# Reordering the last two output tiles of a two-layer graph kernel, and storing one of them through GpSimd's queue

## The chip, the cores and the metric

The kernel runs on one core of a Trainium2 chip. A core has five engines that each work through their own list of instructions: TensorE (PE, matrix products), VectorE (DVE), ScalarE (ACT), GpSimd (POOL) and SyncE (SP, which here only issues transfers). They wait for each other through semaphores. Transfers between the on-chip memory and the chip's main memory are issued from the queues of SP, ACT or POOL and are carried by 16 DMA engines. The metric is the device time of one execution in microseconds (us); less is better.

## The reference, cut to what matters

```python
def _layernorm(x, axis=-1, eps=1e-05):
    m = jnp.mean(x, axis=axis, keepdims=True)
    v = jnp.var(x, axis=axis, keepdims=True)
    return (x - m) / jnp.sqrt(v + eps)

# x: (1354, 512), adj: (1354, 1354), 0/1 with the diagonal set
def _L0_gnn_ref(inst_feature, aggregator_matrix, rel_pair_index, Wq, bq, Wk, bk):
    ...                      # attention scores at 10000 listed pairs, masked by adj, softmax over rows
    return aggregator_factor @ inst_feature

def _L1_gnn_ref(x, adj, weight, bias):
    support = jnp.matmul(x, weight)
    output = jnp.matmul(adj, support)
    return output + bias

x = _layernorm(x + _L0_gnn_ref(x, adj, ...), axis=-1)
x = _layernorm(x + _L1_gnn_ref(x, adj, weight, bias), axis=-1)
```

Everything that this case is about lies in the last line: the sum with the residual `x`, and the normalisation of each row of 512 numbers.

## The kernel before, in words

The 1354 rows are cut into `T` = 11 tiles of `P` = 128 rows (the last has 74), each 512 wide (`H`). The first layer, the handling of the listed pairs and the product of the first layer's result with `adj` fill the first 127 us. Then the output loop starts. It goes over the tiles in the order `OUT_ORDER` = 0 to 4, 10, 5 to 9; in what follows a tile is called by its place in that order, so that "the last tile" is place 10 and "the last but one" is place 9.

For each tile, TensorE makes 12 products with the weights and one that corrects and adds the bias (`weigh`, L1462, and `correct`, L1483). The last tile is cut into columns 0 to 319 and 320 to 511 (`LAST_PARTS`), so that VectorE can start on the first part while TensorE makes the second.

VectorE then does for each tile (L1256 to L1262): the sum with the residual (SCALAR_TENSOR_TENSOR), the statistics (BATCH_NORM_STATS2), and their mean and variance (BATCH_NORM_AGGREGATE). ScalarE takes the root of the variance plus eps (L713). VectorE takes the reciprocal of the root (L905) and multiplies it with minus the mean (L906): these two are `finish_stats`, which gives the scale and the shift. ScalarE normalises the tile in place as scale times value plus shift (L812), and SP issues the store of the tile (L607). ScalarE thus alternates: root of tile t, normalisation of tile t. VectorE calls `finish_stats(t - 1)` after the statistics of tile t.

At the end this differs. For the last tile VectorE makes the sum and the statistics of its first part, then `finish_stats` of the last but one tile (L1276), then the sum and statistics of the second part, the mean and variance (L1279), and `finish_stats` of the last tile (L1280). The last tile is normalised by two engines at once: columns 0 to 255 by ScalarE (L812), columns 256 to 511 by VectorE (L1283). It is stored in two halves of 64 rows, one issued by SP (L610), one by ScalarE (L816). SP at last waits for all stores to land.

GpSimd takes no part in the output loop. Its last work is the scatter of 64 corrected rows (L690), at 121 us; all its transfers before are indirect gathers and scatters (rows chosen by an index).

The buffers of the output tiles are four (`y4`: two halves of `y`, two of `xd`), the statistics sit in `st`, which has two places, taken in turn.

Of the kernel before, what the change touches and what calls it, by code (L numbers as in the profile page):

```python
# [39 lines left out]
BACK_BEFORE = {0: 0, 2: 1, 5: 2, 6: 3}  # L40
SPANS = [(0, 512), (512, 1024), (1024, N)]
UNITS = KF * len(SPANS)
HALF = H // 2
LAST_PARTS = ((0, 320), (320, H))
OUTS = 6
EARLY = 2
# [14 lines left out]
def resnorm_graph(nc, x, adj, pairs, pairs_left, b_qk, w1, b1, adj_t, adj_cols, wq_t, wk_t, adj_diag, out):  # L61
# [5 lines left out]
    with ExitStack() as ctx:  # L67
# [3 lines left out]
        def sem(name):  # L71
            return ctx.enter_context(nc.semaphore(name))
# [180 lines left out]
        qk_read, change_ready, change_T, dT_hi, dT_lo = map(sem, ("qk_read", "change_ready", "change_T", "dT_hi", "dT_lo"))  # L253
        dS_done, right_hi, right_lo = map(sem, ("dS_done", "right_hi", "right_lo"))
        bias_row_loaded, bias_split, biased, ones_laid, out_done, z_ready, z_moments, z_root = map(sem, ("bias_row_loaded", "bias_split", "biased", "ones_laid", "out_done", "z_ready", "z_moments", "z_root"))
        z_stats, z_normed, z_half_normed = map(sem, ("z_stats", "z_normed", "z_half_normed"))

        map_clear, map_idx_ready, map_zeroed, map_marked = map(sem, ("map_clear", "map_idx_ready", "map_zeroed", "map_marked"))
        general_in, rows_in, general_step, early_read = map(sem, ("general_in", "rows_in", "general_step", "early_read"))

        turn = sem("turn")
        out_stored = [sem(f"out_stored{i}") for i in range(4)]
        last_stored = [sem(f"last_stored{i}") for i in range(2)]

        block = ctx.enter_context(nc.Block())

# [21 lines left out]
        def unless_few(eng, name, count, ahead, general):  # L288

            eng.br_lt(count, CAP + 1, on_true=name + "_few", on_false=name + "_many").branch_hint(ahead)  # L290
            with nc.body(name + "_many", valid_engines=[eng.engine]):
                general(eng)
                eng.br(name + "_few")
            nc.switch_bb(name + "_few")
# [235 lines left out]
        def y4(t):  # L530

            return (y if t % 4 < 2 else xd)[:, t % 2, :]
# [9 lines left out]
        @block.sync  # L542
        def _(sp):
            sp.dma_start(ed_i[:], pairs.rearrange("(p c) two -> p c two", p=EP)).then_inc(edges_loaded, 16)
            for g, (a, b) in enumerate(FIRST_PARTS):
                sp.dma_start(stage[:, 0:2, a * P:b * P],  # L546
                             adj_t[0:2].rearrange("t p c -> p t c")[:, :, a * P:b * P]).then_inc(first_loaded[g], 16)
                if g < 3:
                    sp.dma_start(x_sb[:, a:b, :], x[a * P:b * P, :].rearrange("(t p) h -> p t h", p=P)).then_inc(x_loaded[g], 16)
            sp.dma_start(x_sb[:, T - 2, :], rows(x, T - 2)).then_inc(x_loaded[3], 16)  # L550
            sp.dma_start(x_sb[0:64, T - 1, :], x[(T - 1) * P:(T - 1) * P + 64, :]).then_inc(x_loaded[3], 16)
            sp.wait_ge(pad_zeroed, 1)
            sp.dma_start(x_sb[64:LAST, T - 1, :], x[(T - 1) * P + 64:N, :]).then_inc(x_loaded[3], 16)

            def load_adj(t):
                if t >= RING + 2:
                    sp.wait_ge(adj_cast, t - RING - 1)
                elif t >= RING:
                    sp.wait_ge(first_cast, len(FIRST_PARTS))
                sp.dma_start(stage[:, t % RING, :], adj_t[t]).then_inc(adj_loaded[t % RING], 16)  # L560

            load_adj(2)
            sp.wait_ge(edges_split, 2)
            sp.dma_start(row_dram.rearrange("(c p) -> c p", c=LEFT), row16[:]).then_inc(row_stored, 16)
            sp.dma_start(col_dram.rearrange("(c p) -> c p", c=LEFT), col8[:]).then_inc(col_stored, 16)
            load_adj(3)
            load_adj(4)
            load_adj(5)
            load_adj(6)
            sp.wait_ge(row_stored, 16)  # L570
            sp.dma_start(hot[:, :], row_dram.partition_broadcast(P)).then_inc(row_spread, 16)
            load_adj(7)
            sp.wait_ge(col_stored, 16)
            sp.dma_start(cols[:, :], col_dram.partition_broadcast(P)).then_inc(col_spread, 16)
            for t in range(8, T):
                load_adj(t)
            sp.dma_start(bias_row[:, :], b1.rearrange("(o h) -> o h", o=1)).then_inc(bias_row_loaded, 16)
            sp.dma_start(bias_col[:, :, :], b_qk).then_inc(bias_loaded, 16)
            sp.wait_ge(adj_cast, T - 2)
            sp.dma_start(w1_raw, w1.rearrange("(k p) o -> p k o", p=P)).then_inc(w1_loaded, 16)  # L580
            sp.dma_start(wT[:, 0], wq_t.rearrange("(k p) o -> p k o", p=P)).then_inc(wq_loaded, 16)
            sp.dma_start(wT[:, 1], wk_t.rearrange("(k p) o -> p k o", p=P)).then_inc(wk_loaded, 16)
            ahead = sp.mark_branch_hint_location()
            for half in range(2):
                sp.dma_start(adj_tail[EVEN * half:EVEN * half + EVEN, 0:N], adjT[0:EVEN, T - 1, 0:N]).then_inc(tail_laid, 16)
            for t in range(T):
                sp.wait_ge(x1_ready, t + 1)
                sp.dma_start(rows(x1_dram, t), x_sb[0:width[t], t, :]).then_inc(x1_stored, 16)
            sp.wait_ge(odd_zeroed, 1)
            sp.dma_start(x1_odd[CAP:BIAS_ROW, :], x_sb[EVEN:LAST, T - 1, :]).then_inc(odd_in, 16)  # L590
            sp.wait_ge(ones_laid, 1)
            for half in range(2):
                sp.dma_start(stackL[SLOTS * half + CAP:SLOTS * half + BIAS_ROW, 0:N], adjT[EVEN:LAST, T - 1, 0:N]).then_inc(odd_laid, 16)
            sp.wait_ge(bias_split, 2)
            for half in range(2):
                at = SLOTS * half + BIAS_ROW
                sp.dma_start(stackR[at:at + 1, :], bias_hl[:, half, :]).then_inc(biased, 16)
            sp.wait_ge(x1_scattered, 16)
            for n, (a, b) in enumerate(BACK_PARTS):
                if b < T:  # L600
                    sp.dma_start(x_sb[:, a:b, :], x1_dram[a * P:b * P, :].rearrange("(t p) h -> p t h", p=P)).then_inc(x1_back[n], 16)
                else:
                    sp.dma_start(x_sb[0:LAST, a, :], rows(x1_dram, a)).then_inc(x1_back[n], 16)
            unless_few(sp, "sp", slots_wanted(sp), ahead, general_sp)
            for n, t in enumerate(OUT_ORDER[:-1]):
                sp.wait_ge(z_normed, n + 1)
                sp.dma_start(rows(out, t), y4(n)[0:width[t]]).then_inc(out_stored[n % 4], 16)  # L607
            sp.wait_ge(z_normed, T)
            sp.wait_ge(z_half_normed, 1)
            sp.dma_start(rows(out, OUT_ORDER[-1])[0:64, :], y4(T - 1)[0:64, :]).then_inc(last_stored[0], 16)  # L610
            for b in range(4):
                sp.wait_ge(out_stored[b], 16 * len(range(b, T - 1, 4)))
            for half in range(2):
                sp.wait_ge(last_stored[half], 16)


        @block.gpsimd
        def _(pool):
# [73 lines left out]
                in_=q[0:SLOTS, :], in_offset=None, bounds_check=N - 1, oob_is_err=False).then_inc(x1_scattered, 16)  # L692
            pool.wait_ge(x1_scattered, 16)
            unless_few(pool, "pool", slots_wanted(pool), ahead, general_pool)


        @block.scalar
        def _(act):
# [105 lines left out]
            mix_high(11)  # L804
            unless_few(act, "act", slots_wanted(act), ahead, general_act)

            for t in range(T):
                act.wait_ge(z_moments, t + 1)
                root(st[:, t % 2], eps[:]).then_inc(z_root, 1)
                act.wait_ge(z_stats, t + 1)  # L810
                part = y4(t) if t < T - 1 else y4(t)[:, 0:HALF]
                nc.scalar.activation(part, part, ACT.Identity, bias=st[:, t % 2, 9:10],  # L812
                                     scale=st[:, t % 2, 8:9]).then_inc(z_normed, 1)
            act.wait_ge(z_normed, T)
            act.wait_ge(z_half_normed, 1)
            act.dma_start(rows(out, OUT_ORDER[-1])[64:P, :], y4(T - 1)[64:P, :]).then_inc(last_stored[1], 16)  # L816


# [1 line left out]
        def _(dve):  # L820
# [445 lines left out]
            for n, (a, b) in enumerate(LAST_PARTS):  # L1266
                part = y4(t)[:, a:b]
                dve.wait_ge(out_done, T + n)
                V.scalar_tensor_tensor(part, last_bank(n)[:, 0:b - a], 1.0 / WS, x_sb[:, OUT_ORDER[t], a:b],
                                       ALU.mult, ALU.add).then_inc(z_ready, 1)  # L1270
                dve.wait_ge(z_ready, T + n)
                ins = V.bn_stats(last_st[:, 6 * n:6 * n + 6], part)
                if n == 0:
                    ins.then_inc(dve_step, 1)
                    steps += 1
                    finish_stats(T - 2)  # L1276
            step(ins)
            dve.wait_ge(z_normed, t - 1)
            V.bn_aggr(st[:, t % 2, 6:8], last_st[:, 0:12]).then_inc(z_moments, 1)  # L1279
            finish_stats(t)  # L1280
            dve.wait_ge(z_stats, T)
            part = y4(t)[:, HALF:H]
            V.tensor_scalar(part, part, st[:, t % 2, 8:9], st[:, t % 2, 9:10], ALU.mult, ALU.add).then_inc(z_half_normed, 1)  # L1283


        @block.tensor
# [261 lines left out]
```

## Time and profile before

| | us |
|---|---|
| median of 3 runs | 166.4 |
| the 3 runs | 166.4, 167.87, 165.41 |
| the profiled execution's own time | 166.01 |
| its span, from the first to the last instruction | 164.3 |
| granted TensorE clock, mean over the span | 0.991 of full speed |
| busy: TensorE, VectorE, ScalarE, GpSimd | 154.7, 124.5, 74.9, 68.6 |

A line of the timeline reads: start, duration, engine, line of the program, operation, output and input by name, shape, how many; in brackets how long the engine was idle before it and who released it. "SPq" and "ACTq" are issues of transfers on a queue; their duration is that of the issue, not of the transfer. A line of the list of transfers ends with the KB of one and the time from its issue to its landing. A line of the table by stretch gives the stretch, its length, the busy time of PE, PE's weight load, DVE, ACT and POOL with the number of instructions, the granted TensorE clock, the busy share of the DMA engines and the GB/s that they moved. The names `y` and `xd` are output tiles, `st` and `last_st` are statistics, `acc` and `tr` are banks in which TensorE leaves its sums.

### The profile page before, as it was taken

Reading aid. Unit: us, or ns where it says so; the run is one execution under the profiler, and the core shown is the slowest. Engines: PE = TensorE matmul, PEld = TensorE weight load, DVE = VectorE, ACT = ScalarE, POOL = GpSimd, SP = SyncE. Lnnn points to the kernel's source line nnn. Section 1 sums busy time; section 2 is a strip of 40 time slices with the busy share of each in tenths; the row PEclk is TensorE's granted clock in tenths of the full one; section 3 lists DMA queues with packets and bytes.
Section 4 is the critical chain, followed back from the end, with each engine's and each line's share of the span. In section 5 each row is a group of like instructions: output and inputs, shape, how many; then the busy total and the mean of one; then the engine's idle time right before and its main releaser. Section 6 shows DMA issues by size and latency. Waiting matters only on the chain.

```text
span 164.3 us, 2912 instructions
## 1 busy us (share of the span) xinstructions
PE 154.7 (94%) x1029; PEld 81.5 (50%) x1029; DVE 124.5 (76%) x391; ACT 74.9 (46%) x126; POOL 68.6 (42%) x83
## 2 busy tenths in 40 slices
PE   3999999999999999999999999999999999999940
PEld 3964444555454445444454485445764444444530
DVE  2876689997799999999678786898981368666681
ACT  5586639855874312864291253061211204333451
POOL 7787777777777777777306233000030000000000
PEclk9999999999999999999999999999999999999996
DMA  5999979999249999651003720000002972311234
GB/s 126 369 385 335 322 241 363 392 411 339 79 119 345 353 339 394 207 131 42 0 0 94 193 92 6 0 0 0 0 14 51 364 253 86 132 75 66 88 128 128
DMA packets 16232, 28.99 MB, mean 176 GB/s; under 512 B 4769, under 2 KB 5953, under 8 KB 16086
## 3 DMA queue, kind: packets, MB, share of 16 engines
q1 hardware_dynamic: 10742, 24.14, 41.7%
q10 hardware_dynamic: 3280, 3.07, 5.7%
q0 software_dynamic: 2192, 1.57, 4.1%
q8 instruction: 9, 0.15, 0.4%
q14 instruction: 9, 0.07, 0.1%
HBM read 19.83 MB, written 8.58 MB: 173 GB/s over the span
## 4 chain that ended last, share of the span: by engine, by line
PE 61%; DMA 12%; DVE 12%; ACT 6%; SPq 4%; issue 2%; ACTq 0%; DVEq 0%
PE acc L1379 23%; PE acc L1467 13%; PE acc L1311 9%; DMA stage<-in_adj_T 6%; DMA x_sb<-in_x 6%; ACT adjT L702 3%; PE tr L1467 3%; PE tr L1311 3%; DVE st L900 2%; PE tr L1421 2%; PE tr L1457 2%; SPq L546 1%; PE acc L1383 1%; PE acc L1492 1%; PE tr L1325 1%
## 5 line engine op out<-in xcount | busy, mean ns | idle before, releaser
L651 POOL DMA_INDIRECT ed_adj<-in_adj,ed_idx x47 | 47.0, 1001 | 14.5 <-issue 14.0
L1379 PE MATMUL acc<-adjT,x1s 128*128 128x512 f16 (+1 forms) x240 | 49.2, 354 | 0.0
L1311 PE MATMUL acc<-xs,adjT 128*128 128x512 f16 (+1 forms) x176 | 40.2, 379 | 0.0
L1379 PEld LDWEIGHTS acc<-adjT,x1s 128*128 128x128 f16 x240 | 22.7, 98 | 21.1 <-issue 0.2
L1311 PEld LDWEIGHTS acc<-xs,adjT 128*128 128x128 f16 (+1 forms) x176 | 16.5, 98 | 18.9 <-ACT xs L718 0.4
L1467 PE MATMUL acc<-whl,xs 128*128 128x512 f16 (+1 forms) x108 | 23.8, 370 | 0.0
L1467 PEld LDWEIGHTS acc<-whl,xs 128*128 128x128 f16 x108 | 10.6, 98 | 11.8
L1311 PE MATMUL tr<-xs,adjT 128*128 128x512 f16 (+1 forms) x66 | 15.2, 379 | 0.0
L702 ACT CAST adjT<-stage 128x1408 f16<-128x1408 f32 x9 | 12.3, 1361 | 4.0 <-DMA stage<-in_adj_T 3.6
L755 ACT ACTIVATE xs<-acc 128x512 f16<-128x512 f32 (+1 forms) x12 | 6.2, 538 | 9.6 <-PE acc L1383 9.6
L690 POOL DMA_INDIRECT x_dram<-wraw,back_i x1 | 1.3, 1337 | 21.3 <-DVE wraw L1229 21.3
L1311 PEld LDWEIGHTS tr<-xs,adjT 128*128 128x128 f16 (+1 forms) x66 | 6.3, 98 | 7.3
L659 POOL DMA_INDIRECT found<-in_adj,top_i x8 | 8.6, 1070 | 3.0 <-issue 2.1
L873 DVE SCALAR_TENSOR_TENSOR xs<-x_sb,xs 128x512 f16<-128x512 f32 x11 | 7.0, 684 | 3.6 <-ACT xs L718 3.6
L713 ACT ACTIVATE st<-st,co 128x1 f32<-128x1 f32 x11 | 3.2, 292 | 14.0 <-DVE st L901 14.0
L713 ACT ACTIVATE st<-st,eps 128x1 f32<-128x1 f32 x13 | 3.7, 284 | 12.9 <-DVE st L901 12.8
L1292 PE MATMUL tr<-ones 128*128 128x128 f16 x72 | 6.4, 277 | 2.8 <-POOL row_no L632 2.8
L1256 DVE SCALAR_TENSOR_TENSOR y<-acc,x_sb 128x512 f32<-128x512 f32 x5 | 3.5, 692 | 7.1 <-PE acc L1492 7.1
L812 ACT ACTIVATE y<-y,st 128x512 f32<-128x512 f32 x6 | 4.9, 813 | 8.6 <-DVE st L906 8.6
L900 DVE BATCH_NORM_STATS2 st<-y 128x6 f32<-128x512 f32 x12 | 8.3, 695 | 0.4
L718 ACT ACTIVATE xs<-x_sb 128x512 f16<-128x512 f32 x11 | 6.2, 619 | 4.3 <-DMA x_sb<-in_x 4.3
L925 DVE SCALAR_TENSOR_TENSOR xs<-acc,xs 128x512 f16<-128x512 f32 (+1 forms) x12 | 7.2, 619 | 0.9 <-ACT xs L755 0.7
(279 smaller groups left out, 230.7 us busy)
## 6 DMA issues: line engine op xcount, KB each, us to landing
stage<-in_adj_T SPq DMA_DIRECT2D x9, 704.0 KB, 6.5
x_dram<-x_sb SPq DMA_DIRECT2D x10, 256.0 KB
x_sb<-in_x SPq DMA_DIRECT2D x3, 768.0 KB, 7.7
sums_dram<-y ACTq DMA_DIRECT2D x6, 256.0 KB
sums_dram<-xd ACTq DMA_DIRECT2D x5, 256.0 KB, 7.1
x_sb<-x_dram SPq DMA_DIRECT2D x1, 1280.0 KB, 11.8
out<-y SPq DMA_DIRECT2D x5, 256.0 KB, 2.0
stage<-in_adj_T SPq DMA_DIRECT2D x3, 384.0 KB, 5.9
```

Source lines behind the costliest of these rows:

```text
L651: nc.gpsimd.indirect_dma_start(out=ed_adj[0:EP, c:c + 1], out_offset=None, in_=adj_flat, in_offset=bass.IndirectOffsetOnAxis(ap=ed_idx[0:E ...
L659: nc.gpsimd.indirect_dma_start(out=found[0:EP, c:c + 1], out_offset=None, in_=adj_flat, in_offset=bass.IndirectOffsetOnAxis(ap=top_i[0:EP, ...
L702: nc.scalar.copy(adjT[:, :, t * P:(t + 1) * P], stage[:, t % RING, :].rearrange("p (k i) -> p k i", k=T)).then_inc(adj_cast, 1)
L713: return nc.scalar.activation(s[:, 10:11], s[:, 7:8], ACT.Sqrt, bias=floor)
L718: nc.scalar.mul(xs[:, 0, t, :], x_sb[:, t, :], XS).then_inc(x_hi, 1)
L873: V.scalar_tensor_tensor(xs[:, 1, t, :], x_sb[:, t, :], XS, xs[:, 0, t, :], ALU.mult, ALU.subtract).then_inc(x_lo, 1)
L900: step(V.bn_stats(s[:, 0:6], v))
L925: V.scalar_tensor_tensor(mix[:, 1, u % KF, i:j], mix_bank(u)[:, 0:j - i], 1.0 / XS, mix[:, 0, u % KF, i:j], ALU.mult, ALU.subtract).then_i ...
L1292: mm(tr[2][:, 0:P], ones16[:], ones16[:], start=True, stop=True)
L1311: last = mm(sum_bank(i)[:, :], adjT[0:width[k], k, i * P:(i + 1) * P], xs[0:width[k], half, k, :], start=(k == 0 and half == 0), stop=(k = ...
L1379: mm(mix_bank(u)[:, 0:j - i], x1s[:, half, k, f * P:(f + 1) * P], adjT[:, k, i:j], start=(k == 0 and half == 0), stop=False)
L1467: last = mm(bank, mix[:, a, k, t * P:(t + 1) * P], whl[:, b, k, columns], start=(k == 0 and m == 0), stop=False)
```

## The change

Five things change, all in the output loop's end.

VectorE makes the last tile's second sum directly after the first part's statistics; `finish_stats` of the last but one tile goes behind the last tile's mean and variance. The last tile gets no shift any more: VectorE waits for its root, takes the reciprocal and normalises all 512 columns by itself as (value minus mean) times reciprocal. ScalarE takes both last roots first and then normalises the last but one tile, and leaves the last tile alone. The store of the last but one tile goes from SP's queue to GpSimd's. SP and ScalarE still store half of the last tile's rows each.

```diff
@@ SP
-            for n, t in enumerate(OUT_ORDER[:-1]):
+            for n, t in enumerate(OUT_ORDER[:-2]):
                 sp.wait_ge(z_normed, n + 1)
                 sp.dma_start(rows(out, t), y4(n)[0:width[t]]).then_inc(out_stored[n % 4], 16)
-            sp.wait_ge(z_normed, T)
-            sp.wait_ge(z_half_normed, 1)
+            sp.wait_ge(z_last_normed, 1)
             sp.dma_start(rows(out, OUT_ORDER[-1])[0:64, :], y4(T - 1)[0:64, :]).then_inc(last_stored[0], 16)
             for b in range(4):
-                sp.wait_ge(out_stored[b], 16 * len(range(b, T - 1, 4)))
-            for half in range(2):
-                sp.wait_ge(last_stored[half], 16)
+                sp.wait_ge(out_stored[b], 16 * len(range(b, T - 2, 4)))
+            for n in range(3):
+                sp.wait_ge(last_stored[n], 16)
@@ GpSimd
             unless_few(pool, "pool", slots_wanted(pool), ahead, general_pool)
+            n, t = T - 2, OUT_ORDER[T - 2]
+            pool.wait_ge(z_normed, n + 1)
+            nc.gpsimd.dma_start(rows(out, t), y4(n)[0:width[t]]).then_inc(last_stored[2], 16)
@@ ScalarE
-            for t in range(T):
+            def z_root_of(t):
                 act.wait_ge(z_moments, t + 1)
                 root(st[:, t % 2], eps[:]).then_inc(z_root, 1)
+
+            def z_norm_of(t):
                 act.wait_ge(z_stats, t + 1)
-                part = y4(t) if t < T - 1 else y4(t)[:, 0:HALF]
-                nc.scalar.activation(part, part, ACT.Identity, bias=st[:, t % 2, 9:10],
+                nc.scalar.activation(y4(t), y4(t), ACT.Identity, bias=st[:, t % 2, 9:10],
                                      scale=st[:, t % 2, 8:9]).then_inc(z_normed, 1)
-            act.wait_ge(z_normed, T)
-            act.wait_ge(z_half_normed, 1)
+
+            for t in range(T - 2):
+                z_root_of(t)
+                z_norm_of(t)
+            z_root_of(T - 2)
+            z_root_of(T - 1)
+            z_norm_of(T - 2)
+            act.wait_ge(z_last_normed, 1)
             act.dma_start(rows(out, OUT_ORDER[-1])[64:P, :], y4(T - 1)[64:P, :]).then_inc(last_stored[1], 16)
@@ VectorE
                 if n == 0:
                     ins.then_inc(dve_step, 1)
                     steps += 1
-                    finish_stats(T - 2)
             step(ins)
             dve.wait_ge(z_normed, t - 1)
             V.bn_aggr(st[:, t % 2, 6:8], last_st[:, 0:12]).then_inc(z_moments, 1)
-            finish_stats(t)
-            dve.wait_ge(z_stats, T)
-            part = y4(t)[:, HALF:H]
-            V.tensor_scalar(part, part, st[:, t % 2, 8:9], st[:, t % 2, 9:10], ALU.mult, ALU.add).then_inc(z_half_normed, 1)
+            finish_stats(T - 2)
+            dve.wait_ge(z_root, T)
+            step(V.reciprocal(st[:, t % 2, 8:9], st[:, t % 2, 10:11]))
+            V.tensor_scalar(y4(t), y4(t), st[:, t % 2, 6:7], st[:, t % 2, 8:9], ALU.subtract, ALU.mult).then_inc(z_last_normed, 1)
```

VectorE, from the last tile's first sum to the end of its list. `xd` is the last tile, `last_st` its statistics, `acc` and `tr` the banks of its two parts. Before:

```order
L1269 SCALAR_TENSOR_TENSOR xd<-acc,x_sb 128x320 [waits out_done,out_stored2]
L1272 BN_STATS last_st<-xd 128x6 [waits z_ready]
L905 RECIPROCAL st<-st 128x1 [waits z_root]
L906 TENSOR_SCALAR st<-st 128x1 [waits dve_step]
L1269 SCALAR_TENSOR_TENSOR xd<-tr,x_sb 128x192 [waits out_done]
L1272 BN_STATS last_st<-xd 128x6 [waits z_ready]
L1279 BN_AGGR st<-last_st 128x2 [waits z_normed,dve_step]
L905 RECIPROCAL st<-st 128x1 [waits z_root]
L906 TENSOR_SCALAR st<-st 128x1 [waits dve_step]
L1283 TENSOR_SCALAR xd<-xd,st 128x256 [waits z_stats]
```

After, in the changed program's own line numbers:

```order
L1277 SCALAR_TENSOR_TENSOR xd<-acc,x_sb 128x320 [waits out_done,out_stored2]
L1280 BN_STATS last_st<-xd 128x6 [waits z_ready]
L1277 SCALAR_TENSOR_TENSOR xd<-tr,x_sb 128x192 [waits out_done]
L1280 BN_STATS last_st<-xd 128x6 [waits z_ready]
L1286 BN_AGGR st<-last_st 128x2 [waits z_normed,dve_step]
L913 RECIPROCAL st<-st 128x1 [waits z_root]
L914 TENSOR_SCALAR st<-st 128x1 [waits dve_step]
L1289 RECIPROCAL st<-st 128x1 [waits z_root]
L1290 TENSOR_SCALAR xd<-xd,st 128x512 [waits dve_step]
```

The last but one tile's reciprocal and shift moved from before the second sum to behind the last tile's mean and variance; the last tile's own shift is gone, and its normalisation covers 512 columns.

ScalarE, from the last but one tile's root to the end. Before:

```order
L713 ACTIVATE st<-st,eps 128x1 [waits z_moments]
L812 ACTIVATE y<-y,st 128x512 [waits z_stats]
L713 ACTIVATE st<-st,eps 128x1 [waits z_moments]
L812 ACTIVATE xd<-xd,st 128x256 [waits z_stats]
L816 DMA out<-xd 64x512 [waits z_half_normed,z_normed]
```

After:

```order
L714 ACTIVATE st<-st,eps 128x1 [waits z_moments] x2
L814 ACTIVATE y<-y,st 128x512 [waits z_stats]
L824 DMA out<-xd 64x512 [waits z_last_normed]
```

Both roots now stand ahead of the last but one tile's normalisation (`y`), and the normalisation of the last tile (`xd`) left this engine.

## Rows read from the trace of the kernel before

**Rows 1.** The page: busy time, share and instructions of each engine.

```profile
PE 154.7 (94%) x1029; PEld 81.5 (50%) x1029; DVE 124.5 (76%) x391; ACT 74.9 (46%) x126; POOL 68.6 (42%) x83
```

**Rows 2.** The page: the chain that ended last, by engine.

```profile
PE 61%; DMA 12%; DVE 12%; ACT 6%; SPq 4%; issue 2%; ACTq 0%; DVEq 0%
```

**Rows 3.** Timeline from 157.2 us: the last two tiles.

```profile
157.27 0.81 ACT L812 ACTIVATE y<-y,st 128x512 f32<-128x512 f32 x1 [1.81 <-DVE st L906]
157.66 0.49 DVE L1272 BATCH_NORM_STATS2 last_st<-xd 128x6 f32<-128x320 f32 x1
...
157.85 0.25 PE L1492 MATMUL tr<-stackR,stackL 128*128 128x192 f16 x1
157.99 0.28 ACT L713 ACTIVATE st<-st,eps 128x1 f32<-128x1 f32 x1
...
158.30 0.17 DVE L905 RECIPROCAL st<-st 128x1 f32<-128x1 f32 x1
158.50 0.21 DVE L906 TENSOR_SCALAR st<-st 128x1 f32<-128x1 f32 x1
158.63 0.35 DVE L1269 SCALAR_TENSOR_TENSOR xd<-tr,x_sb 128x192 f32<-128x192 f32 x1
158.75 0.81 ACT L812 ACTIVATE y<-y,st 128x512 f32<-128x512 f32 x1 [0.48 <-DVE st L906]
159.01 0.36 DVE L1272 BATCH_NORM_STATS2 last_st<-xd 128x6 f32<-128x192 f32 x1
159.41 0.21 DVE L1279 BATCH_NORM_AGGREGATE st<-last_st 128x2 f32<-128x12 f32 x1
159.65 0.29 ACT L713 ACTIVATE st<-st,eps 128x1 f32<-128x1 f32 x1
159.98 0.17 DVE L905 RECIPROCAL st<-st 128x1 f32<-128x1 f32 x1 [0.36 <-ACT st L713]
160.18 0.21 DVE L906 TENSOR_SCALAR st<-st 128x1 f32<-128x1 f32 x1
160.43 0.60 ACT L812 ACTIVATE xd<-xd,st 128x256 f32<-128x256 f32 x1 [0.48 <-DVE st L906]
160.43 0.41 DVE L1283 TENSOR_SCALAR xd<-xd,st 128x256 f32<-128x256 f32 x1
161.05 0.56 SPq L610 DMA_DIRECT2D out<-xd  x1
161.06 0.56 ACTq L816 DMA_DIRECT2D out<-xd  x1
```

**Rows 4.** Timeline of SP's queue from 159.3 us: the last but one store.

```profile
159.59 0.33 SPq L607 DMA_DIRECT2D out<-y  x1
```

**Rows 5.** Transfers: direction, queue, kind, count, KB of one, us to landing.

```profile
out<-y SPq DMA_DIRECT2D x5, 256.0 KB, 2.0
...
out<-xd SPq DMA_DIRECT2D x1, 128.0 KB, 2.4
out<-xd ACTq DMA_DIRECT2D x1, 128.0 KB, 2.7
...
wraw<-sums_dram,slot_i POOLq DMA_INDIRECT x1, 3.9
```

**Rows 6.** By stretch: the last but one store's data on the DMA engines.

```profile
160.80:161.10 0.30, 0.00 (x0) 0.00 (x0) 0.04 (x1) 0.23 (x1) 0.00 (x0) 1.00 0.95 375
```

**Rows 7.** Timeline, 86 to 88 us: GpSimd's first gather of rows.

```profile
86.67 0.17 DVE L1085 CAST slot_i<-slot 128x2 int32<-128x2 f32 x1
87.11 0.94 POOL L664 DMA_INDIRECT wraw<-in_x,slot_i  x1 [7.83 <-DVE slot_i L1085]
```

**Rows 8.** That gather's line (128 rows of 2 KB): time from issue to landing.

```profile
DMA to landing us min/median/max: 3.3/3.3/3.3
```

**Rows 9.** Timeline, 119 to 122 us: GpSimd's scatter and its releaser.

```profile
119.66 0.55 DVE L1229 TENSOR_SCALAR wraw<-wraw,st 128x512 f32<-128x512 f32 x1
...
121.19 1.34 POOL L690 DMA_INDIRECT x_dram<-wraw,back_i  x1 [21.27 <-DVE wraw L1229]
```

More of the change, by code:

```diff
@@ L42 @@
 UNITS = KF * len(SPANS)
-HALF = H // 2
 LAST_PARTS = ((0, 320), (320, H))
@@ L255, in resnorm_graph @@
         bias_row_loaded, bias_split, biased, ones_laid, out_done, z_ready, z_moments, z_root = map(sem, ("bias_row_loaded", "bias_split", "biased", "ones_laid", "out_done", "z_ready", "z_moments", "z_root"))
-        z_stats, z_normed, z_half_normed = map(sem, ("z_stats", "z_normed", "z_half_normed"))
+        z_stats, z_normed, z_last_normed = map(sem, ("z_stats", "z_normed", "z_last_normed"))
         map_clear, map_idx_ready, map_zeroed, map_marked = map(sem, ("map_clear", "map_idx_ready", "map_zeroed", "map_marked"))
@@ L262, in resnorm_graph @@
         out_stored = [sem(f"out_stored{i}") for i in range(4)]
-        last_stored = [sem(f"last_stored{i}") for i in range(2)]
+        last_stored = [sem(f"last_stored{i}") for i in range(3)]
         block = ctx.enter_context(nc.Block())
```

## The prediction

> **What bounds the kernel now.** I read the busy shares first: TensorE is busy for 154.7 of 164.3 us, 94% [rows 1], so for most of the span nothing but TensorE counts, and the change doesn't touch it. The chain of waits says the same with one addition: TensorE has 61% of it, VectorE 12% and ScalarE 6% [rows 2]. So VectorE and ScalarE count only where TensorE has nothing left to do. The timeline shows that place. TensorE's last product ends at 157.85 + 0.25 = 158.10 us [rows 3], and the span ends at 164.3 us. The last 6.2 us are a tail without TensorE, and the whole change lies in it. Whatever it does is worth a part of 6.2 us in 166, that is at most 3.7%, and nothing that any row suggests comes near that.
>
> The tail has two pieces. The first is a chain of small instructions on VectorE and ScalarE, up to 161.05 us, where SP and ScalarE issue the two halves of the last tile's store [rows 3]. The second is the store itself: ScalarE's half takes longer, 2.7 us to landing [rows 5], so it lands at 161.06 + 2.7 = 163.76 us. From there to the end of the span are 0.54 us, in which SP's last wait falls and the program ends; I keep these 0.54 us behind whichever store lands last. The reader should see one more thing in the rows: the last but one tile is normalised at 158.75 + 0.81 = 159.56 us and its store goes out at 159.59 us [rows 3, 4]. With 2.0 us to landing [rows 5] it is down at 161.59 us, over 2 us before the end. This tile has slack before, and the change spends it.
>
> **The second sum moves ahead.** Before, it starts at 158.63 us, behind a reciprocal that had to wait for ScalarE's root (157.99 + 0.28 = 158.27) and a shift. Without these two it can start when the first part's statistics end, 157.66 + 0.49 = 158.15, and when TensorE's last product is there, 158.10 [rows 3]. With the 0.02 us that the rows show between dependent instructions I take 158.17: 0.46 us earlier. TensorE stands right behind this: were VectorE earlier still, nothing would be gained.
>
> The rest of the chain keeps the distances of rows 3. Statistics 0.38 us behind the sum: 158.55. Mean and variance 0.40 behind that: 158.95. The root 0.24 behind: 159.19. ScalarE is free by then, since its last root ended at 158.27 and no normalisation stands between any more. The mean and variance also wait for the normalisation that ends at 157.27 + 0.81 = 158.08; it has long ended. The reciprocal comes 0.33 behind the root, at 159.52.
>
> **The last tile's shift goes, VectorE normalises alone.** Before, from reciprocal to shift 0.20 us, from shift to normalisation 0.25 us, and ScalarE's half took 0.60 us, VectorE's 0.41 us, so ScalarE's set the end [rows 3]. Now the normalisation follows the reciprocal by the 0.20 us that a step on VectorE takes: 159.72. It has 512 columns. A row of the same operation, shape and two scalars from memory took 0.55 us [rows 9]; that is no guess between bounds, though it would be 0.82 us if twice the 256 columns took twice the time. So it ends at 160.27, and the stores go out 0.02 later at 160.29 us, against 161.05: 0.76 us earlier, of which 0.46 came from the sum, 0.25 from the shift, and 0.05 from 0.55 against 0.60 us. ScalarE's issue has to go behind its normalisation of the other tile, below, and so at 160.34 us at the worst; I leave this 0.05 us in the rounding. With 2.7 us to landing the last tile is down at 162.99 us.
>
> **The last but one tile.** Its reciprocal and shift go behind the last tile's mean and variance. An independent instruction follows at 0.13 us (the sum behind the shift, 158.50 to 158.63), so the reciprocal is at 159.08, the shift 0.20 later at 159.28, and it ends at 159.49, just before 159.52, where the last tile's reciprocal wants VectorE. It is hidden under ScalarE's root; if that cover is missed by the 0.03 us that is left, it costs as much. ScalarE's normalisation starts 0.25 behind the shift, at 159.53 (its second root ends at 159.48), and ends at 160.34 us, 0.78 us later than before.
>
> **Its store through GpSimd.** This is the term that no row shows: GpSimd has issued only indirect transfers. Two durations are needed. From the release to the start of the issue: 0.27 us at the first gather (86.67 + 0.17 to 87.11 [rows 7]), 0.98 us at the scatter (119.66 + 0.55 to 121.19 [rows 9]); at best nothing. From the start to landing: a gather of the same 256 KB in rows of 2 KB took 3.3 us [rows 8], another 3.9 us, and a store of 256 KB from SP's queue 2.0 us [rows 5]. A gain below 2.0 us is excluded, since the bytes are the same and go the same way. I take the nearest rows, both from the one gather that found GpSimd idle, as this store will: 0.27 + 3.3 = 3.57 us. The bounds are 2.0 and 0.98 + 3.9 = 4.88 us. The store lands at 160.34 + 3.57 = 163.91 us.
>
> The three stores share the DMA engines. These moved 375 GB/s while the last but one store's data passed before [rows 6], which makes 0.70 us for 256 KB. The last tile's data would be delayed by that at most, to 163.69 us, still ahead of GpSimd's store; and I expect no overlap, for GpSimd's data should come later.
>
> **The sum.** The later landing is 163.91 us; with 0.54 us the span is 164.45 us, 0.15 us more than before. The 0.76 us won on the last tile are spent by the last but one, whose landing takes over the end. Against the profiled execution's own 166.01 us this gives **166.2 us**. That execution is 0.4 us below the median of the three runs, 166.4 us, and the three spread over 2.5 us (165.41 to 167.87), more than the whole effect. About 2%, 3.3 us, is what a measurement of this kernel can tell from no change.
>
> **Rival 1: GpSimd's store is quick and the last tile sets the end.** A plain store needs no index for each row, and the writing of descriptors, 0.94 us of the gather [rows 7], may shrink. For this to decide, release to landing must stay under 162.99 - 160.34 = 2.65 us. The span is then 162.99 + 0.54 = 163.53 us, the time 165.2 us. For it speaks that SP's plain store needs 2.0 us; against it, that every transfer of this queue with a landing shown took at least 3.3 us. The Trainium skill, page "DMA: Bandwidth & Descriptors", section "Latency and other measured facts", puts the first byte of a transfer of GpSimd's queue only some 0.4 us behind one of the other queues, and the section "Anatomy of one DMA — SWDGE (gpsimd) path" fits about 2.0 us plus the bytes at 436 GB/s: an estimate from that page is 2.6 us for these 256 KB, which would just fall under this rival. No row of this trace shows a plain store on that queue, and the gathers of rows 5 and 8 lie above it.
>
> **Rival 2: slower, because GpSimd wakes late and writes its descriptors late.** The place is the same store; the price is the other end of the bounds, 4.88 us, and it decides from 163.76 - 160.34 = 3.42 us on, where its landing passes that of before. Span 160.34 + 4.88 + 0.54 = 165.76 us, time 167.5 us, 0.9% slower. For it: the last transfer that GpSimd issued had this long start. Against: that row has an extra index bound to load ahead, and a scatter's descriptors took 1.34 us against 0.94 for a gather. My own forecast is the mild end of this mechanism, with 0.15 us past the threshold.
>
> **Rival 3: the move doesn't happen as drawn.** If TensorE's last product is seen by VectorE later than 158.10 (its ends are modelled), the second sum starts late by that; at 158.63, as before, the 0.46 us are gone. Then the last tile lands at 163.45, the last but one at 164.37, and the time is 166.6 us. The idle gaps after other tiles speak against it.
>
> **Chances.** The forecast (GpSimd's store sets the end, release to landing 3 to 4 us) has 0.45: nearest rows. Rival 1 has 0.27, rival 2 0.18, rival 3 0.06, and 0.04 is left for what I don't see, 0.02 beyond 2% on either side. Low end: rival 1's 165.2 less a little for the runs' spread, 165.1. High end: the forecast plus the spread of the runs above the profiled one, and the half of rival 2 up to 0.6% slower, 167.1. Faster by over 2% has 0.02, slower by over 2% 0.02 (it would take 164.3 + 3.3 - 0.54 - 160.34 = 6.7 us from release to landing), within 2% 0.96.
>
> **What the changed profile would show.** The second sum 0.02 us behind the first part's statistics, and no earlier than TensorE's last product. Reciprocal, shift, reciprocal on VectorE between the mean and variance and the root's return, without a gap that is longer than the 0.57 us of before. A normalisation of 512 columns of about 0.55 us, the stores of the last tile about 0.76 us earlier against TensorE's end, that is 2.2 us behind it. The last but one tile's normalisation ending within 0.1 us of the last one's. A GpSimd issue 0.3 us behind it, of about 0.9 us, and its landing as the last one. The prediction is wrong if SP's last wait ends on the last tile's halves (rival 1), if a GpSimd issue starts later than 0.5 us after its release or lands over 4 us behind (rival 2), or if ScalarE's store is held up behind its normalisation by more than 0.1 us.

## The result, and the profile after

| | before | after |
|---|---|---|
| median of 6 runs, us | 166.09 (165.41 to 168.22) | 169.24 (168.43 to 169.96) |
| ratio after to before | | 1.019, 95% interval 1.015 to 1.023 |
| span of the profiled execution, us | 164.3 | 167.3 |
| end of TensorE's last product, us | 158.10 | 158.26 |
| **tail**: from there to the end of the span, us | 6.2 | 9.04 |

The change makes the kernel slower by 1.9%, about 3.2 us. The forecast was 166.2 us with 165.1 to 167.1 as its range; the time lies outside. Of the 3.0 us by which the two spans differ, 0.16 us stand ahead of TensorE's end and 2.84 us in the tail. I use the tail for everything below, since what lies ahead of it moves from one execution to the next: the kernel before and e2_pool_only (below) run the same instructions up to there, and TensorE's last product ends at 158.10 us in one trace and at 160.14 us in the other. Each tail is read from one profiled execution; what repeats between kernels, as the 2.16 or 2.17 us to the last tile's stores, repeats within 0.01 us.

The timeline of the changed kernel's last two tiles answers to [rows 3]. Its columns are those of before; line numbers are those of the changed program.

```profile
157.82 0.49 DVE L1280 BATCH_NORM_STATS2 last_st<-xd 128x6 f32<-128x320 f32 x1
...
158.01 0.25 PE L1499 MATMUL tr<-stackR,stackL 128*128 128x192 f16 x1
...
158.29 0.36 DVE L1277 SCALAR_TENSOR_TENSOR xd<-tr,x_sb 128x192 f32<-128x192 f32 x1
158.69 0.36 DVE L1280 BATCH_NORM_STATS2 last_st<-xd 128x6 f32<-128x192 f32 x1
159.08 0.21 DVE L1286 BATCH_NORM_AGGREGATE st<-last_st 128x2 f32<-128x12 f32 x1
159.21 0.11 DVE L913 RECIPROCAL st<-st 128x1 f32<-128x1 f32 x1
159.32 0.29 ACT L714 ACTIVATE st<-st,eps 128x1 f32<-128x1 f32 x1 [0.90 <-DVE st L1286]
159.35 0.21 DVE L914 TENSOR_SCALAR st<-st 128x1 f32<-128x1 f32 x1
159.60 0.81 ACT L814 ACTIVATE y<-y,st 128x512 f32<-128x512 f32 x1
159.65 0.16 DVE L1289 RECIPROCAL st<-st 128x1 f32<-128x1 f32 x1
159.85 0.55 DVE L1290 TENSOR_SCALAR xd<-xd,st 128x512 f32<-128x512 f32 x1
160.42 0.56 SPq L608 DMA_DIRECT2D out<-xd  x1
160.43 0.57 ACTq L824 DMA_DIRECT2D out<-xd  x1
160.71 0.61 POOL L695 DMA_DIRECT2D out<-y  x1 [38.01 <-ACT y L814]
```

Up to the issues this is what was forecast: the last tile's stores go out 160.42 - 158.26 = 2.16 us behind TensorE's end, where before it was 161.05 - 158.10 = 2.95 us. So 0.79 us were won; the forecast had 0.76. What comes behind the issues ate them and more. First the landings, in the list of transfers of the changed kernel (it answers to [rows 5]; the last number is us from issue to landing):

```profile
out<-y POOLq DMA_DIRECT2D x1, 256.0 KB, 3.8
...
out<-xd SPq DMA_DIRECT2D x1, 128.0 KB, 2.7
out<-xd ACTq DMA_DIRECT2D x1, 128.0 KB, 4.2
```

GpSimd's store lands at 160.71 + 3.8 = 164.51 us, 6.25 us into the tail; the forecast had 5.81. ScalarE's half of the last tile, 2.7 us before, now needs 4.2 us: it lands at 164.63, the last of all. And from there to the end of the span are not 0.54 us but 2.7. The waits of SP's queue show that SP is done and waits for another engine at the program's end (engine and line that waited, what for, total us, times, longest):

```profile
SPq L612 <- DMA out<-xd: 3.6, 2, 2.2
SPq L66 <- PEq L66: 2.3, 1, 2.3
```

In the kernel before, the second of these waits was 0.2 us long. The row names TensorE's queue (PEq), but TensorE had long been done. Which engine it is, the line of the program's closing block tells. Its rows give the queue, the instruction, its length in ns (least, median, most), and when it starts. Before, L67:

```profile
L67 POOLq EVENT_SEMAPHORE  x2: 17/17/17, 164.1 to 164.2; - x2
L67 POOLq DRAIN  x1: 5042/5042/5042, 126.2 to 126.2; - x1
...
L67 ACTq DRAIN  x1: 646/646/646, 161.7 to 161.7; - x1
...
L67 SPq DRAIN  x1: 7/7/7, 164.0 to 164.0; - x1
```

After, L66:

```profile
L66 POOLq EVENT_SEMAPHORE  x2: 17/17/17, 167.1 to 167.2; - x2
...
L66 POOLq DRAIN  x1: 6372/6372/6372, 160.7 to 160.7; - x1
L66 ACTq DRAIN  x1: 645/645/645, 161.0 to 161.0; - x1
...
L66 SPq DRAIN  x1: 7/7/7, 165.0 to 165.0; - x1
```

Every engine closes its list with a DRAIN, and the closing EVENT_SEMAPHOREs of all come when the last DRAIN is through. GpSimd's takes 5.04 us. Before, GpSimd came to it at 126.2 us, and nobody noticed. After, GpSimd comes to it only with its store, at 160.7 us; it is through at 160.7 + 6.37 = 167.07, and the span ends at 167.3. SP's own drain began at 165.0. No row of the profile's page names a DRAIN; it shows only when the closing block's line is asked for.

### The profile page after: what moved, and what is told of

It reads as the page before. It is cut to its first block, busy times and chain, and to the rows that moved or that the text cites. A ratio compares the mean times of both kernels' runs of the same rounds, so it can differ in the third digit from the quotient of the medians.

```text
span 167.3 us, 2907 instructions
## 1 busy us (share of the span) xinstructions
PE 155.1 (93%) x1028; PEld 82.1 (49%) x1029; DVE 124.8 (75%) x390; ACT 74.3 (44%) x125; POOL 69.5 (42%) x84
## 4 chain that ended last, share of the span: by engine, by line
PE 46%; issue 25%; DVE 14%; POOL 5%; DMA 5%; POOLq 1%; DVEq 0%
PE acc L1318 17%; PE acc L1386 9%; PE tr L1318 9%; POOL found L657 4%; PE tr L1299 4%; DMA found<-in_adj,top_i 3%; PE tr L1304 2%; DMA x_dram<-wraw,back_i 2%; DVE st L908 2%; PE tr L1428 2%; DVE xs L933 1%; DVE y L957 1%; DVE hot L927 1%; PE tr L1332 1%; PE tr L1441 0%
## 5 line engine op out<-in xcount | busy, mean ns | idle before, releaser
L695 POOL DMA_DIRECT2D out<-y x1 | 0.6, 612 | 38.0 <-ACT y L814 38.0
L1299 PE MATMUL tr<-ones 128*128 128x128 f16 x72 | 7.1, 293 | 2.8 <-POOL row_no L630 2.8
L1299 PEld LDWEIGHTS tr<-ones 128*128 128x128 f16 x72 | 6.9, 140 | 2.8 <-POOL row_no L630 2.8
```

Source lines behind the costliest of these rows:

```text
L1299: mm(tr[2][:, 0:P], ones16[:], ones16[:], start=True, stop=True)
```

## The experiments

Theories at the start: **A**, GpSimd's closing drain costs about 5 us whenever it starts; **B**, it lasts until some 2.6 us behind the landing of GpSimd's store; **C**, the three stores get in each other's way, and the drain is only a shadow. All tails are read like that of the table above (start of TensorE's last product, plus its length, to the end of the span); "last tile issued" is the later of its issues, "landing" the latest one of all, issue plus time to landing; "drain ends" is GpSimd's closing one. All four are in us behind TensorE's end. Each ratio is to runs of the kernel before taken together with it.

| kernel | last tile issued | landing | drain ends | tail | ratio to before, 95% interval |
|---|---|---|---|---|---|
| before | 2.95 | 5.66 | long before | 6.2 | |
| after | 2.16 | 6.37 | 8.8 | 9.04 | 1.019 (1.015 to 1.023) |
| e1_sp_store | 2.55 | 5.35 | long before | 6.0 | 0.999 (0.995 to 1.002) |
| e2_pool_only | 2.95 | 5.65 | 7.5 | 7.66 | 1.008 (1.004 to 1.012) |
| e3_late_memset | 2.55 | 5.35 | 7.3 | 7.56 | 1.005 (1.001 to 1.009) |
| e4_wait_landing | 2.16 | 6.36 | 11.5 | 11.74 | one run |
| e5_early_drain | 2.17 | 6.27 | 6.2 | 6.83 | 1.004 (1.001 to 1.007) |
| e6_early_drain_memset | 2.56 | 5.36 | 2.4 | 5.99 | one run |
| e8_whole_stores | 2.17 | 4.88 | long before | 5.31 | 0.995 (0.992 to 0.998) |
| e9_pool_earlier | 2.16 | 4.88 | 3.2 | 5.39 | 0.995 (0.992 to 0.999) |
| e10_drain_count | 2.17 | 4.89 | long before | 5.34 | one run |
| e11_two_stores_drain | 2.16 | 5.05 | 5.2 | 5.61 | 0.998 (0.995 to 1.002) |
| e12_pool_only_drain | 2.95 | 5.65 | 4.3 | 6.24 | 0.999 (0.995 to 1.002) |
| e13_halves_one_queue | 2.77 | 6.47 | 6.4 | 7.01 | one run |

Runs of one kernel scatter by 1.3 to 2.5 us. The ratios part e2 from e1, but e3 from neither of them; the intervals agree with the tails (1.46 us more tail in e2 are 0.9%), and the tails carry the verdicts. All the experiments differ from the kernel before by less than 1%; where there is one run only, its time says nothing and its tail alone is used.

**e1_sp_store**, against the changed kernel:

```diff
 # SP
+            sp.wait_ge(z_normed, T - 1)
+            sp.dma_start(rows(out, OUT_ORDER[T - 2]), y4(T - 2)[0:width[OUT_ORDER[T - 2]]]).then_inc(last_stored[2], 16)
             sp.wait_ge(z_last_normed, 1)
 # GpSimd
-            pool.wait_ge(z_normed, n + 1)
-            nc.gpsimd.dma_start(rows(out, t), y4(n)[0:width[t]]).then_inc(last_stored[2], 16)
```

> The changed kernel with the last but one tile's store back on SP's queue, ahead of SP's half of the last tile; GpSimd does nothing in the output loop. The measure is the tail, from the end of TensorE's last product to the end of the span: 6.2 us before, 9.0 us with the change. Theory A (the closing drain on GpSimd's list holds the end, 6.4 us behind its store) and theory B (that drain ends some 2.6 us behind the landing of GpSimd's store) both expect a tail of about 5.6 us: GpSimd's drain is over long before, SP issues at 2.2 and 2.5 us, lands 2.4 to 2.7 us later, 0.5 us of ending. About 0.6 us faster than before. Theory C (the three stores are in each other's way, and ScalarE's half lands 4.2 us behind its issue because of it) expects 4.2 us to landing here too and a tail of 6.9 us.

Measured: tail 6.0 us. The loss is gone with GpSimd's store, so the new order on VectorE and ScalarE is not its cause. Only 0.2 us of the expected 0.6 are left as a gain: SP's half of the last tile is issued behind the other store at 2.55 us and takes 2.8 us to land. ScalarE's half lands in 2.8 us, not 4.2, although three stores cross here as well:

```profile
out<-xd ACTq DMA_DIRECT2D x1, 128.0 KB, 2.8
out<-xd SPq DMA_DIRECT2D x1, 128.0 KB, 2.8
```

Three stores on the queues of SP and ScalarE don't explain the 4.2, so C in its simple form is wrong.

**e2_pool_only**, the kernel before with one edit, the last but one tile's store on GpSimd's queue.

> The kernel before with one edit: the last but one tile's store goes from SP's queue to GpSimd's; VectorE and ScalarE as before. The tile is ready at 1.5 us of the tail, GpSimd issues at 1.8. Theories A and B: the drain ends 6.4 us behind that, a tail of 8.3 us, about 2.1 us slower than before, although this store lands (3.8 us behind its issue, at 5.6) no later than the last tile's. Theory C: the stores don't meet as closely, tail 6.2 to 6.7 us.

Measured: tail 7.66 us, 1.46 us more than before. ScalarE's half lands when it did, in 2.7 us, and GpSimd's store ahead of it:

```profile
out<-y POOLq DMA_DIRECT2D x1, 256.0 KB, 2.4
```

The drain ends 7.5 us into the tail. Here the drain is the whole loss. I had expected 8.3, as the drain took 6.37 us with the change; it takes 5.70 us here:

```profile
L67 POOLq DRAIN  x1: 5701/5701/5701, 161.9 to 161.9; - x1
```

Its row starts with the store's own issue, which takes GpSimd 0.61 us, so 5.09 us are left for the drain alone, against 5.76 with the change.

**e3_late_memset**, e1_sp_store with late work on GpSimd that is no transfer:

```diff
 # GpSimd, at its end
+            pool.wait_ge(z_normed, T - 1)
+            nc.gpsimd.memset(probe[:], 0.0)
```

> As e1_sp_store, but GpSimd waits for the last but one tile's normalisation and then sets 128 numbers of a scratch tile to zero: late work on GpSimd, no transfer. Theory A (the drain costs about 5 us whenever it starts, as in the trace of before where nothing was in flight): it starts at 2.2 us of the tail and ends at 7.3, tail 7.5 us, 1.9 us longer than e1_sp_store. Theory B (the drain waits for transfers): nothing is in flight, tail as e1_sp_store, 5.6 us.

```profile
163.75 0.10 POOL L697 MEMSET probe<- 128x1 f32 x1 [37.80 <-ACT y L816]
```

```profile
L66 POOLq DRAIN  x1: 5103/5103/5103, 163.7 to 163.7; - x1
```

Measured: tail 7.56 us against 7.5 (A) and 5.6 (B). The first row is of the timeline, the second of the closing block. One memset of 0.10 us costs 1.56 us at the end, with no transfer of GpSimd in flight for 38 us. B is wrong. (This profiled execution took 170.83 us against a median of 167.32; TensorE ended late in it, and only distances in its tail are used. The medians of e3 and e1, 167.32 and 166.15 us, differ the same way, by 1.2 us.)

**e4_wait_landing**, the changed kernel with `pool.wait_ge(last_stored[2], 16)` behind GpSimd's store.

> The changed kernel, with GpSimd waiting for its own store to land before it comes to the end of its list. The store lands at 6.3 us of the tail. Theory A: a drain of 5.0 us starts only then, tail 11.5 us, 2.5 us longer than with the change. Theory B: the drain has nothing left to wait for but the same 2.6 us behind the landing, tail 9.0 us as with the change; or, if that rest is not part of waiting, 7 us.

```profile
L66 POOLq DRAIN  x1: 5057/5057/5057, 165.8 to 165.8; - x1
```

Measured: tail 11.74 us. The store has landed when the drain starts, and the drain takes its 5.06 us all the same. A holds where nothing is in flight: the drain's start sets the end.

**e5_early_drain** and **e6_early_drain_memset** ask what these 5 us are paid for: for having issued transfers at all (A1), or for those issued since the last drain (A2). Both add one line behind GpSimd's scatter at 126 us, the first to the changed kernel, the second to e3_late_memset:

```diff
             unless_few(pool, "pool", slots_wanted(pool), ahead, general_pool)
+            nc.gpsimd.drain()
```

> The changed kernel with an extra drain on GpSimd at 126 us, right after its last gather and scatter work, where nothing waits for it. Theory A1 (a drain costs 5 us once GpSimd has issued any transfer in the program): the closing drain stays at about 5.7 us behind the store's descriptors, tail 9.0 us as with the change. Theory A2 (a drain pays for the transfers issued since the last drain; before, 60 of them): the closing drain has one store to pay for, so little more than its landing: tail about 7 us, 2 us less than with the change.

> e3_late_memset with the same extra drain at 126 us. Between the two drains GpSimd issues no transfer at all. A1: the closing drain takes 5.0 to 5.1 us again, tail 7.7 us. A2: it takes 0.2 us, like the one at the program's start (0.18 us), tail 5.9 us.

The closing block of e5_early_drain, then its extra drain (L693); under it the two of e6_early_drain_memset:

```profile
L66 POOLq DRAIN  x1: 3781/3781/3781, 160.5 to 160.5; - x1
...
L693 POOLq DRAIN  x1: 5047/5047/5047, 126.8 to 126.8; - x1
```

```profile
L66 POOLq DRAIN  x1: 173/173/173, 159.7 to 159.7; - x1
...
L696 POOLq DRAIN  x1: 5041/5041/5041, 125.4 to 125.4; - x1
```

A2 holds. In e6 the early drain takes the 5.04 us, and the closing one 0.17 us. In e5 the closing one has one store behind it and is through at 160.5 + 3.78 = 164.3 us, as that store lands (160.53 + 3.7 = 164.23). It is so in e11, e12 and e13 too, where the closing drain ends 0.1 us behind that landing. The tail falls from 9.04 to 6.83 us. One hidden instruction takes back 2.2 of the 2.84 us.

**e10_drain_count** has the extra drain between GpSimd's 55 lookups and its last 5 transfers; the rest is e8_whole_stores, below.

> e8_whole_stores with a drain on GpSimd behind the 47 and 8 lookups and ahead of its 5 last transfers (two gathers of rows, the gather of sums, the gather of columns, the scatter). Theory D1 (the cost goes with the number of transfers since the last drain): this drain takes some 4.6 us, plus what the last lookup still needs to land, and the closing one 0.17 + 5 x 0.08 = 0.6 us. D2 (any transfer since the last drain costs the whole 5 us): both take about 5.0 us. D3 (the cost is that of the gathers with long rows or of the scatter, not of the lookups): the first is short, the closing one near 5 us. The tail is that of e8_whole_stores, 5.3 us, in all three.

```profile
L66 POOLq DRAIN  x1: 529/529/529, 128.2 to 128.2; - x1
...
L661 POOLq DRAIN  x1: 16451/16451/16451, 69.4 to 69.4; - x1
```

D1: with 5 transfers since the last drain the closing one takes 0.53 us (expected 0.6), with 60 it takes 5.04, with none 0.17. That is (5.04 - 0.53) / 55 = 0.08 us for each transfer and (0.53 - 0.17) / 5 = 0.07, though the 5 move far longer rows than the 55; so it isn't the bytes. Each lookup addresses 128 rows and the last 5 transfers 64 or 128, so that a price for each transfer and a price for each row can't be told apart here. The first drain's row starts with the queue of lookups and can't be read for its price.

**e12_pool_only_drain**, e2_pool_only with the early drain.

> e2_pool_only with the extra drain at 126 us. The store of the last but one tile is issued by GpSimd at 1.8 us of the tail and lands at 4.2, the last tile's at 5.6 as in the kernel before. Theory A2 (a drain pays for the transfers since the last one, and waits for its own to land): the closing drain ends at the landing, 4.2, nothing is behind it, and the tail is 6.2 us as before: the 1.5 us that e2_pool_only lost are all the drain's.

Measured: tail 6.24 us against 6.2 expected. With the drain paid for early, moving the store to GpSimd costs nothing here, where 1.2 us lie between its issue and those of the halves, and GpSimd's store lands in 2.4 us.

**e8_whole_stores** goes after the landing, and for a better kernel. Against the changed one, GpSimd stores nothing, and:

```diff
 # SP
-            sp.dma_start(rows(out, OUT_ORDER[-1])[0:64, :], y4(T - 1)[0:64, :]).then_inc(last_stored[0], 16)
+            sp.dma_start(rows(out, OUT_ORDER[-1]), y4(T - 1)[0:P, :]).then_inc(last_stored[0], 16)
 # ScalarE
-            act.wait_ge(z_last_normed, 1)
-            act.dma_start(rows(out, OUT_ORDER[-1])[64:P, :], y4(T - 1)[64:P, :]).then_inc(last_stored[1], 16)
+            act.wait_ge(z_normed, T - 1)
+            act.dma_start(rows(out, OUT_ORDER[T - 2]), y4(T - 2)[0:width[OUT_ORDER[T - 2]]]).then_inc(last_stored[1], 16)
```

> The changed kernel with both last stores on the hardware queues, each whole: SP stores the last tile, ScalarE the last but one; GpSimd stores nothing. Issues at 2.2 us of the tail on both. If only GpSimd's drain and its store's crossing with the others cost time, the landing is some 2.9 us later (512 KB at 340 to 375 GB/s are 1.4 to 1.5 us) and the tail is 5.6 us, 0.6 us less than before and 3.4 less than with the change. If the three-store crossing of e1_sp_store is about bytes and not queues, the tail is 6.0 us as there.

Measured: tail 5.31 us (5.6 expected), 0.9 us less than before, ratio 0.995 with an interval clear of 1, by median 165.64 against 166.30 us. It has the shortest tail of this study; e9_pool_earlier, below, is as fast by its runs. The new order on VectorE and ScalarE is worth its gain once both stores are whole and on the queues of SP and ScalarE. Against e1_sp_store, which has the same order, the latest landing is 0.47 us earlier (4.88 against 5.35), of which 0.38 is the last issue: no store stands behind another. The issue rows tell part of it: a store of 128 rows takes SP 0.33 us to issue, one of 64 rows 0.56 (with the change, above). And whole tiles move faster. By stretch of 0.4 us (the last three numbers: TensorE's clock, busy share of the DMA engines, GB/s), the changed kernel:

```profile
161.46:161.86 0.40, 0.00 (x0) 0.00 (x0) 0.00 (x0) 0.00 (x0) 0.00 (x0) 1.00 0.61 138
161.86:162.26 0.40, 0.00 (x0) 0.00 (x0) 0.00 (x0) 0.00 (x0) 0.00 (x0) 1.00 1.04 154
162.26:162.66 0.40, 0.00 (x0) 0.00 (x0) 0.00 (x0) 0.00 (x0) 0.00 (x0) 0.75 0.76 215
162.66:163.06 0.40, 0.00 (x0) 0.00 (x0) 0.00 (x0) 0.00 (x0) 0.00 (x0) 0.50 0.94 328
...
163.86:164.26 0.40, 0.00 (x0) 0.00 (x0) 0.00 (x0) 0.00 (x0) 0.00 (x0) 0.50 0.08 31
```

and e8_whole_stores:

```profile
162.39:162.79 0.40, 0.00 (x0) 0.00 (x0) 0.00 (x0) 0.00 (x0) 0.00 (x0) 1.00 0.47 184
162.79:163.19 0.40, 0.00 (x0) 0.00 (x0) 0.00 (x0) 0.00 (x0) 0.00 (x0) 1.00 0.99 394
163.19:163.59 0.40, 0.00 (x0) 0.00 (x0) 0.00 (x0) 0.00 (x0) 0.00 (x0) 1.00 0.95 374
```

Both move 512 KB. With halves in play the engines are fully busy and move 154 GB/s; with two whole tiles they move 394. GpSimd's store isn't needed for this: in the kernel before, where the two halves are alone on the engines, these are busy for 94% and move 179 GB/s:

```profile
162.50:162.90 0.40, 0.00 (x0) 0.00 (x0) 0.00 (x0) 0.00 (x0) 0.00 (x0) 0.50 0.94 179
```

The changed kernel's last row shows one more thing. While its last two landings are still to come, at 164.51 and 164.63 us, the 16 engines are busy for 8% on the mean: the late end isn't one in which all of them are full.

**e9_pool_earlier**, e8_whole_stores with the store of place 7 on GpSimd's queue.

> e8_whole_stores with one store on GpSimd's queue again, but that of place 7, ready 2.8 us ahead of TensorE's end. Theory A: the issue starts at -2.5 us, descriptors take 0.6, the drain 5.1: it ends 3.2 us into the tail, hidden, and the tail is as in e8_whole_stores. If a store on GpSimd's queue costs by itself, wherever it stands, it is longer.

Measured: tail 5.39 us against 5.31, ratio 0.995 as well. A store on GpSimd's queue is free if the drain behind it ends in time; it ended at 3.2 us, as expected.

**e11_two_stores_drain**, e5_early_drain with the last tile stored whole by SP.

> e5_early_drain with the last tile stored whole by SP and no store by ScalarE: two stores instead of three at the end, SP's at 2.2 us of the tail and GpSimd's at 2.5. If it is ScalarE's queue that GpSimd's store holds back (4.2 us to landing with the change, 2.7 to 2.8 without a store by GpSimd), SP's whole store lands in 2.0 to 2.8 us and GpSimd's in 3.7 us sets the end: tail 6.5 us. If GpSimd's store holds back whatever shares the DMA engines with it, SP's store lands in about 4 us and the tail is 6.8 us as in e5_early_drain.

Measured: SP's store lands in 2.0 us, GpSimd's in 2.6 instead of 3.7, tail 5.61 us. Neither expectation held (6.5 and 6.8 us). It is 1.2 us less than in e5_early_drain, and the difference is that the last tile goes whole on one queue instead of in halves on two. So GpSimd's store doesn't hold back whatever shares the engines with it.

**e13_halves_one_queue**, e5_early_drain with both halves issued by SP.

> e5_early_drain with both halves of the last tile's store issued by SP, one behind the other, and none by ScalarE; GpSimd stores the last but one tile. In e5_early_drain ScalarE's half lands 4.1 us behind its issue, in e11_two_stores_drain (one whole store by SP) everything lands within 2.6. If it is the cut into halves of 64 rows that meets GpSimd's store badly, a half lands about 4 us behind its issue here too and the tail is 6.8 us or more. If it takes three queues at once (SP, ScalarE, GpSimd), both halves and GpSimd's store land within 3 us and the tail is 5.6 to 5.9 us.

Measured: SP's first half lands in 2.8 us, its second in 3.7, GpSimd's store in 3.9, tail 7.01 us. The slow landing is there with two queues, so it doesn't take three at once. It is there with two halves close beside GpSimd's store, and not with halves alone (before), with halves beside a whole store by SP (e1), with halves 1.2 us behind GpSimd's store (e2, e12), or with one whole store beside it (e11). No run puts two whole stores beside GpSimd's, so the cut and the number of stores aren't parted, and how the halves come to land late isn't shown.

## Why the prediction was wrong, point by point

- **What bounds the kernel, and where the change acts**: right. TensorE's end moved by 0.16 us, the tail by 2.84. But the tail's 6.2 us, 3.7%, limit only what can be won; a loss has no such limit.
- **Second sum, shift, normalisation**: right. The sum starts 0.03 us behind TensorE's end (0.07 forecast), the 512 columns take 0.55 us as the row of the same shape said, the issues come 0.79 us earlier (0.76 forecast). TensorE's end does stand right behind the sum. Rival 3 fell.
- **The last but one tile's normalisation**: right. It ends 159.60 + 0.81 - 158.26 = 2.15 us into the tail, 2.24 forecast, and its reciprocal and shift did fit under the root.
- **Release to start of GpSimd's issue**: 0.30 us, 0.27 forecast. Rival 2's late wake didn't come.
- **Landing of GpSimd's store**: 3.8 us against 3.3, mis-sized by 0.5. Away from the halves the plain store is quick: 2.4 us in e2_pool_only, e9_pool_earlier and e12_pool_only_drain. The Trainium skill, page "DMA: Bandwidth & Descriptors", section "Anatomy of one DMA — SWDGE (gpsimd) path", gave an estimate of 2.6 us; these runs agree with it, and my nearest row, an indirect gather, was the worse guide. Beside two halves it is 3.7 to 3.9 us. The prediction held this estimate, which counts from the issue, against rival 1's 2.65 us, which count from the release: with the 0.27 us between them it is 2.87 us and misses that bound, as the 0.30 + 2.4 = 2.7 us of e2_pool_only do.
- **"The three stores share the DMA engines"**: wrong in size. I allowed at most 0.70 us of delay and expected none, from the rate of a whole store, 375 GB/s; the trace before has 179 GB/s for the halves. ScalarE's half was 4.2 - 2.7 = 1.5 us later. This alone turned the 0.79 us won into 0.7 us lost; e5_early_drain, which has the slow landing and no late drain, shows it as a tail of 6.83 us against 6.2. Its ratio of 1.004, which makes 166.8 us of 166.09, is still inside the forecast's range.
- **"I keep these 0.54 us behind whichever store lands last"**: this is the step that failed. It treats the end of the program as a fixed rest behind the last landing. Where GpSimd's drain is through by the last landing or just behind it, this rest measures 0.4 to 0.7 us; with work at GpSimd's end the end comes behind the later of that and GpSimd's drain. The drain added 9.04 - 6.83 = 2.2 us, three quarters of the loss. None of the rivals had it. The row that shows it, a DRAIN of 5042 ns on GpSimd's queue at 126.2 us, stands in the trace of the kernel before. I read busy times and waits of the engines, and left out the closing block.

The ledger of the tail: 6.2 - 0.79 (issues) + 1.5 (ScalarE's half lands late) - 0.1 (it lands in 4.1 us in e5_early_drain, in 4.2 with the change) = 6.8, + 2.2 (drain, as the difference between the two) = 9.0 us.

What stays open: why the closing drain with the change takes 5.76 us behind the store's issue and 5.09 in e2_pool_only, whether the drain's price goes by transfers or by rows, and why halves of 64 rows close beside a GpSimd store land late.

## What to carry to other kernels

Before giving an idle engine the last piece of work, look at what its list still has to do to end the program: here 5 us of drain were free at 126 us and cost 2.2 us at 161. If a GpSimd that has issued many transfers must do something late, drain it once in a hidden place before, and look again whether the late transfer is worth it: the two best kernels of this study, e8 and e9, keep the new order and leave GpSimd out of the tail. Two stores of whole tiles, one for each of the queues of SP and ScalarE, were down sooner than a whole one and two halves on the same queues (4.88 against 5.35 us).

## What the runs showed of the hardware that I had not expected

- GpSimd's DRAIN takes 0.17 us with no transfer of its own since the last drain, 0.53 us with 5, 5.04 us with 60, all of them landed: about 0.08 us for each of these indirect ones. A plain store added 0.02 us when landed (e4_wait_landing, 5.06 us). After an early drain, with one store still in flight, it lasted until 0.1 us behind the landing (e5, e11, e12, e13). The late work need not be a transfer: a memset of 0.10 us had a drain of 5.10 us behind it.
- An early drain resets that bill: 5.04 us at 125.4 us, then 0.17 us at the end (e6_early_drain_memset).
- A plain store of 256 KB on GpSimd's queue lands 2.4 us behind the start of its issue, which takes 0.61 us; an indirect gather of the same size took 3.3 [rows 8], with an issue of 0.94 us [rows 7].
- A store of 64 rows takes SP 0.56 us to issue where one of 128 rows takes 0.33. Two such halves move 179 GB/s at engines busy for 94% (before), and 138 to 215 GB/s in the first 1.2 us with the change, where whole tiles reach 394.
